# A windowed-attention block with an MLP: attention rewritten in unit slots, with projections and heads in groups of four units

## The reference

```python
h = layernorm(x, norm1_g, norm1_b)                 # over 48 channels
hw = windows(h)                                    # 1024 windows of 64 tokens
qkv = hw @ qkv_w + qkv_b                           # 3 heads of 16
attn = softmax((q * 16 ** -0.5) @ k.T + bias)      # bias by relative position
out = (attn @ v) @ proj_w + proj_b
x = x + unwindow(out)
h2 = layernorm(x, norm2_g, norm2_b)
return x + gelu(h2 @ fc1_w + fc1_b) @ fc2_w + fc2_b   # 192 hidden
```

## Time and profile before

| | us |
|---|---|
| median of 3 runs | 1205.87 |
| lowest and highest run | 1198.97, 1209.87 |
| profiled execution | 1205.63 |
| its span | 1203.9 |

### The profile page before, as it was taken

How to read it: one execution, slowest core, us unless ns; L and a number is a source line. 1 busy time by engine, 2 the same in 40 slices (tenths; PEclk the granted TensorE clock), 3 DMA queues, 4 the chain that set the end, 5 groups by cost and what they waited for, 6 DMA issues and landing times.

```text
span 1203.9 us, 29333 instructions
## 1 busy us (share of the span) xinstructions
PE 1079.1 (90%) x7622; PEld 964.3 (80%) x7622; DVE 873.9 (73%) x2751; ACT 896.8 (74%) x2755; POOL 759.7 (63%) x1173
## 2 busy tenths in 40 slices
PE   2998889888988889888889888888889999999997
PEld 1887777777777777777777777777779999999997
DVE  3567777777777777777777767777767777777773
ACT  2578777888888788888877888888777767667664
POOL 3555566565556656555566555556668888888882
PEclk9989999999999999999999999999989999999999
DMA  1000000100000010000000100000001111111111
GB/s 49 16 26 27 26 26 28 38 31 32 29 26 26 26 34 33 32 31 26 26 26 30 36 31 32 28 26 26 14 14 39 39 39 40 46 45 39 39 39 53
DMA packets 24744, 38.26 MB, mean 32 GB/s; under 512 B 4055, under 2 KB 20634, under 8 KB 24730
## 3 DMA queue, kind: packets, MB, share of 16 engines
q1 hardware_dynamic: 24730, 38.10, 10.0%
HBM read 25.50 MB, written 12.58 MB: 32 GB/s over the span
## 4 chain that ended last, share of the span: by engine, by line
PE 54%; ACT 23%; issue 12%; DVE 6%; POOL 3%; SPq 1%; DMA 1%; DVEq 0%; POOLq 0%; ACTq 0%
PE scores_ps L586 14%; ACT k_blocks L752 7%; PE kv_ps L509 4%; ACT v_blocks L763 4%; PE mixed_ps L539 4%; ACT tokens_t L740 4%; PE q_ps L515 4%; PE kv_ps L516 4%; ACT probs L768 3%; PE scores_ps L523 3%; PE turn_ps L550 3%; PE kv_ps L579 3%; PE turn_ps L563 2%; PE heads_t_ps L550 2%; POOL lowered L449 2%
## 5 line engine op out<-in xcount | busy, mean ns | idle before, releaser
L449 POOL TENSOR_TENSOR lowered<-biased,row_top 128x384 f32<-128x384 f32 x256 | 212.1, 828 | 355.0 <-DVE row_top L972 354.9
L523 PE MATMUL scores_ps<-k_blocks,q_blocks 96*128 96x192 f32 x1024 | 232.7, 351 | 42.2 <-DVE q_blocks L960 27.1
L752 ACT ACTIVATE k_blocks<-kv_ps 32x128 f32<-32x128 f32 x768 | 203.6, 265 | 64.0 <-PE kv_ps L516 58.0
L363 POOL TENSOR_TENSOR rstd<-small,minus_half 128x4 f32<-128x4 f32 (+1 forms) x160 | 243.3, 1527 | 0.0
L523 PEld LDWEIGHTS scores_ps<-k_blocks,q_blocks 96*128 96x128 f32 x1024 | 164.3, 194 | 64.2 <-issue 35.5
L968 DVE TENSOR_TENSOR biased<-scores_ps,pos 128x384 f32<-128x384 f32 x256 | 142.8, 558 | 96.1 <-PE scores_ps L523 89.9
L539 PEld LDWEIGHTS mixed_ps<-v_blocks,probs_t 128*128 128x128 f32 x1536 | 196.2, 195 | 15.6 <-issue 1.9
L539 PE MATMUL mixed_ps<-v_blocks,probs_t 128*128 128x66 f32 x1536 | 205.5, 271 | 0.9 <-ACT probs_t L745 0.9
L586 PEld LDWEIGHTS scores_ps<-wfc,hidden 128*128 128x128 f32 x1536 | 181.1, 192 | 5.4
L586 PE MATMUL scores_ps<-wfc,hidden 128*128 128x96 f32 x1536 | 179.9, 274 | 0.0
L972 DVE TENSOR_REDUCE row_top<-biased 128x6 f32<-128x384 f32 x256 | 141.6, 553 | 8.9
(11 more groups left out here) (106 smaller groups left out, 1888.2 us busy)
## 6 DMA issues: line engine op xcount, KB each, us to landing
x_in<-in_x SPq DMA_DIRECT2D x256, 48.0 KB
x<-in_x SPq DMA_DIRECT2D x128, 96.0 KB
out<-x SPq DMA_DIRECT2D x128, 96.0 KB
pos_in<-in_L_conv_rel_bias_table SPq DMA_DIRECT2D x8, 10.6 KB
wfc_in<-in_L_conv_fc_w SPq DMA_DIRECT2D x2, 36.0 KB
wqkv_in<-in_L_conv_qkv_w SPq DMA_DIRECT2D x2, 27.0 KB
wfc<-in_L_conv_fc_w SPq DMA_DIRECT2D x2, 24.0 KB
gains<-in_L_conv_norm_g SPq DMA_DIRECT2D x2, 0.2 KB
```

The lines of the kernel that those rows point to most:

```text
L363: pool.tensor_tensor(rstd[:, groups], small[:, 7, groups], minus_half[:, groups], ALU.pow).then_inc(step, 1)
L449: pool.tensor_tensor(lowered[:, k % 2, :, :], biased[:, k % 2, :, :], broadcast(row_top[:, k % 2, :], 2, TOK), ALU.subtract).then_inc(lowe ...
L523: mm = pe.matmul(bank[:, at:at + HEADS * TOK], q_blocks[:, k % 2, a, :, :].rearrange("p b q -> p (b q)"), k_blocks[:, k % 2, a, :, :].rear ...
L752: ins = act.activation(k_blocks[rows, k % 2, :, h, :], kv_ps[rows, at:at + 2 * TOK].rearrange("p (a t) -> p a t", a=2), ACT.Copy)
```

## The change

Attention is written anew on all engines; the MLP stage keeps its instructions and only takes other banks.

- Q, K and V are made for a group of four units: one matmul of 512 columns for Q, one for K, four for V. q_blocks, k_blocks and v_blocks hold two groups. `k_out` is three activations of 512 elements per group, `v_out` two of 384, `q_out` one of 1024.
- q_ps, kv_ps, turn_ps and heads_t_ps become four banks x_ps that rotate among the tokens, Q, K, V, transposed heads and the heads projection.
- `probs_t_out` is one activation of 384 elements.
- `normalise` is done for two units at once (a mixed_ps of two units), `turn_heads` and `heads_out` for four.
- In slot k TensorE does scores(k), turn_probs(k-2), one filling (`fill`), mix(k-2). ScalarE has exp(k-1) ahead of probs_t_out(k-2).
- GpSimd's preparation of the next batch begins in slot 6 of the batch before; SyncE loads x_in two batches ahead.
- wproj is loaded in the order of the new heads layout (six DMAs in place of two, and no masking on VectorE). The remaining preparation of weights moves from ahead of the first scores into slot 5 of the first batch.

The core of the diff; its `body` functions are, in this order, those of SyncE, GpSimd, TensorE, ScalarE and VectorE.

```diff
-        q_blocks = sb("q_blocks", [C2, 2, 2, 2, TOK])
-        k_blocks = sb("k_blocks", [C2, 2, 2, HEADS, TOK])
-        v_blocks = sb("v_blocks", [128, V_BUFS, HEADS, MIX])
+        q_blocks = sb("q_blocks", [C2, 2, UNITS, 2, 2, TOK])
+        k_blocks = sb("k_blocks", [C2, 2, UNITS, 2, HEADS, TOK])
+        v_blocks = sb("v_blocks", [128, 2, UNITS, HEADS, MIX])
...
+        x_ps = [ps(f"x_ps{i}") for i in range(4)]
+        turn2_ps = x_ps[1]
+        fc1_ps = [x_ps[2], x_ps[0], probs_t_ps]
...
+            sp.wait_ge(small_step, 10)
+            load_front(1)
+            def body(n, more):
+                if more:
+                    sp.wait_ge(small_step, FRONT_STEPS * (n + 1) + 10)
+                    load_front(n + 2)
                 wait(sp, x2_ok, 2 * n)
...
+            def body(n, first, last, more):
                 for k in range(QUADS):
                     lower(QUADS * n + k, k)
+                    if first and k == 1:
+                        front_sums(1)
+                        front_centre(1)
+                    if k == (2 if first else 0) and not last:
+                        front_root(0, 0)
+                        front_root(0, 1)
+                    if k == (2 if first else 1) and not last:
+                        front_root(1, 0)
+                        front_root(1, 1)
+                    if k == (3 if first else 2) and not last:
+                        front_scale(n + 1, 0)
+                        front_scale(n + 1, 1)
+                    if k == 6 and more:
+                        front_sums(n + 2)
+                    if k == 7 and more:
+                        front_centre(n + 2)
...
+            def project_q(bank, part):
+                pe.matmul(bank[0:C2, :], wqkv[:, 0:C2], group_tokens(part), start=True, stop=True).then_inc(q_mm, 1)
...
+            def fill(n, k, first, last):
+                if k == 0:
+                    wait(pe, x2_ok, 2 * n - 2)
+                    project_q(x_ps[0], 1)
+                    if not first:
+                        wait(pe, heads_ok, 4 * n - 2)
+                        turn_heads(x_ps[1], 0)
+                if k == 1:
+                    project_k(x_ps[2], 1)
+                if k == 2:
+                    wait(pe, v_ok, 2 * n + 1)
+                    project_v(x_ps[3], 1)
+                if k == 3:
+                    if not first:
+                        wait(pe, k_ok, 2 * n + 2)
+                        wait(pe, heads_ok, 4 * n)
+                        turn_heads(x_ps[2], 1)
+                    if not last:
+                        wait(pe, q_ok, 2 * n + 2)
+                        wait(pe, normed_ok, 2 * n + 3)
+                        turn_tokens(0)
+                        wait(pe, heads_t_ok, 2 * n - 1)
                         wait(pe, normed_ok, 2 * n + 4)
                         turn_tokens(1)
+                if k == 4:
+                    wait(pe, v_ok, 2 * n + 2)
...
+                        wait(pe, heads_t_ok, 2 * n)
+                        project_heads(x_ps[3], 0)
+                if k == 5:
...
+                        wait(pe, tokens_ok, 2 * n + 4)
+                        project_q(x_ps[1], 0)
+                        wait(pe, k_ok, 2 * n + 2)
+                        project_k(x_ps[2], 0)
+                if k == 6 and not first:
+                    project_heads(x_ps[0], 1)
+                if k == 7:
...
+                        wait(pe, x2_ok, 2 * n - 1)
+                        project_v(x_ps[3], 0)
+            def body(n, first, last):
+                s0 = QUADS * n
+                for k in range(QUADS):
+                    if k % UNITS == 0:
+                        wait(pe, q_ok, 2 * n + k // UNITS + 1)
+                        wait(pe, k_ok, 2 * n + k // UNITS + 1)
+                    wait(pe, biased_ok, s0 + k - 1)
+                    scores(k)
+                    if not (first and k < 2):
+                        turn_probs_of(s0 + k - 2, k)
+                    fill(n, k, first, last)
+                    if not (first and k < 2):
+                        wait(pe, probs_t_ok, s0 + k - 1)
+                        if k % 2 == 0:
+                            wait(pe, heads_ok, 4 * n + k // 2 - 1)
+                        if k == 2:
+                            wait(pe, v_ok, 2 * n + 1)
+                        mix(k - 2)
...
+            def k_out(part):
                 for h in range(HEADS):
                     rows = slice(2 * HD * h, 2 * HD * h + 2 * HD)
+                    ins = act.activation(k_blocks[rows, part, :, :, h, :].rearrange("p u a t -> p (u a) t"),
+                                         x_ps[2][rows, :].rearrange("p (ua t) -> p ua t", t=TOK), ACT.Copy)
                 ins.then_inc(k_ok, 1)
...
             def body(n, first, last):
+                s0 = QUADS * n
                 for k in range(QUADS):
+                    if not (first and k == 0):
+                        exp_of(s0 + k - 1, (k - 1) % QUADS)
                     if not (first and k < 2):
+                        wait(act, probs_turned, s0 + k - 1)
                         probs_t_out()
+                    if k == 0:
+                        wait(act, v_mm, 2 * n + 1)
+                        v_out(0)
+                    if k == 1 and not first:
+                        wait(act, heads_turned, 2 * n - 1)
+                        heads_out(x_ps[1], 0)
+                    if k == 2:
+                        wait(act, k_mm, 2 * n + 2)
+                        k_out(1)
+                    if k == 3:
+                        wait(act, v_mm, 2 * n + 2)
+                        v_out(1)
+                        if not first:
+                            wait(act, heads_turned, 2 * n)
+                            heads_out(x_ps[2], 1)
+                    if k == 4 and not last:
+                        for half in range(2):
+                            wait(act, turned, 2 * n + 3 + half)
+                            tokens_out(half)
+                    if k == 6:
...
+                            wait(act, k_mm, 2 * n + 3)
+                            k_out(0)
...
             def body(n, first, last, more):
+                s0 = QUADS * n
                 for k in range(QUADS):
+                    if k % 2 == 0 and not (first and k < 4):
+                        if k % UNITS == 0:
+                            wait(dve, heads_turned, 2 * n - 2 + k // UNITS)
+                        wait(dve, mixed_mm, s0 + k - 2)
+                        normalise(4 * n + k // 2 - 2, 1 - k // UNITS, k % UNITS)
+                    wait(dve, scores_mm, s0 + k + 1)
+                    top(s0 + k, k)
...
+                    if k == 1:
+                        wait(dve, q_mm, 2 * n + 2)
+                        q_out(x_ps[0], 1)
...
+                    if more and k in (4, 5):
+                        stats_front(n + 2, k - 4)
+                    if k == 5 and not first:
+                        dve.wait_ge(res_loaded, 64 * n)
+                        add_proj(n - 1, x_ps[3], 0)
+                    if k == 5 and first:
+                        other_weights()
+                    if k == 6:
...
+                            wait(dve, q_mm, 2 * n + 3)
+                            q_out(x_ps[1], 0)
+                    if k == 7 and not first:
+                        add_proj(n - 1, x_ps[0], 1)
```

More of the change, by code:

```diff
@@ L518, in scores, with project_k, project_v @@
+            def project_k(bank, part):
+                pe.matmul(bank[0:C2, :], wqkv[:, C2:2 * C2], group_tokens(part), start=True, stop=True).then_inc(k_mm, 1)
+            def project_v(bank, part):
+                for u in range(UNITS):
+                    mm = pe.matmul(bank[:, C2 * u:C2 * u + C2], tokens_t[:, UNITS * part + u, :], wqkv[:, 2 * C2:3 * C2],
+                                   start=True, stop=True)
+                mm.then_inc(v_mm, 1)
             def scores(k):
-                bank = scores_ps[k % 2]
+                part, u = divmod(k, UNITS)
@@ L630, in body @@
-                    if not (first and k < 3):
-                        if k == 3:
-                            wait(pe, x2_ok, 2 * n)
-                        turn_heads_of(g0 + k - 3, k - 3)
-                    if first and k == 2:
-                        wait(pe, weights_ok, 1)
-                    if not (first and k < 2):
-                        wait(pe, heads_ok, g0 + k - 2)
-                        mix(g0 + k - 2, k - 2)
-                    if k == 5 and not last:
-                        wait(pe, normed_ok, 2 * n + 3)
-                        turn_tokens(0)
@@ L646, in body @@
-                    if k == 5 and last:
+                if k == 4:
+                    wait(pe, v_ok, 2 * n + 2)
+                    if first:
+                        wait(pe, weights_in, 16 * WEIGHT_DMAS)
+                        pe.matmul(x_ps[3][:, 0:HID], fc1_shift[:, :], wfc1_in[0:C, :], start=True, stop=True
+                                  ).then_inc(bias_mm, 1)
+                    else:
```

(15 more changed lines are left out.)

419 lines of the change are left out of this document (153 added, 266 removed).

## The result

The changed kernel took 1118.01 us, median of 4 runs (1115.94 to 1121.09), beside 1202.42 us for the kernel before in the same series (4 runs, 1198.19 to 1209.87): ratio 0.929, 95% interval 0.924 to 0.935. The forecast was 1122 us. The profiled execution took 1117.6 us with a span of 1115.8.

The account below looks back on a forecast made before the run. Attention was taken as bound by TensorE's in-order queue plus its standstills. From 1205.6 us, 81 for steady batches and 2.6 for the start were subtracted, with nothing for drain and MLP: 1122 us, range 1095 to 1170.

Parts of the forecast that it names:

- The main term: Steady attention batches: period falls from 26.53 to 23.7 us, 2.8 us a batch over 29 batches, 81 us.
- The walk through the eight slots: Steady batch: slot lengths added up from instruction prices and latencies, carrying late engines over, sum 23.4 us.
- I add 0.3 for stops that the walk does not see: Steady batch: allowance of 0.3 us for unseen stops, raising the period from 23.4 to 23.7 us.
- Here GpSimd decides: Slot 3, turn of tokens: GpSimd's 13.4 us of work since slot 6 sets when tokens come; slot length 3.78 us.
- The ScalarE term: ScalarE in a steady batch: fewer, larger copies bring its work to 17.0 us; K from 3.2 to 1.8 per four units.
- 2.6 us won: Start: first biased 3 us later, but batch 0 then loses less; net 2.6 us won, bounds -6 and +5.
- The last batch and the drain keep their chains: End of attention: statistics, roots and transposes keep their chains, so no change, +-5 us.
- (a): Attention slots: late GpSimd or VectorE makes the exponential delay the probabilities' copy, 0.2 us a slot; period 25.2, 1164 us; chance 0.18.
- (b): Steady batches: the stalls go altogether, period near 22.5 us, total 1087 us; chance 0.07.
- (c): ScalarE's big copies cost 1108 ns like scattered 512-element writes; period 26.6, about 1203 us, no gain; chance 0.06.
- (d): Attention: new short stops make TensorE's clock fall once per batch, 4.3 us each; period 28.0, 1246 us; chance 0.09.
- The stop of VectorE for x_in: Sign of being wrong: VectorE waiting for input DMA at its statistics; lateness there was priced at nothing.

Follow-up runs that it names:

- Run 4: Changed kernel with Q and K of the next batch's first group projected and copied in slot 7 instead of slot 5: 1163.56 us, ratio 0.968.
- Run 3: Changed kernel with two of the four GpSimd roots per batch left out, so part of the tokens' normalisation is not computed: 1118.10 us, ratio 0.930.
- run 9: Changed kernel with only VectorE's copy of Q for the second group moved from slot 1 to slot 2: 1113.97 us, ratio 0.927.
- run 12: Changed kernel with the second group's Q copied in slot 2 and, in the drain, the last pair normalised before the rest of the second tokens: 1110.50 us, ratio 0.924.
- run 2: Changed kernel with K copied in twelve activations of 128 elements per group instead of three of 512: 1132.43 us, ratio 0.942.
- run 5: Kernel before with only larger ScalarE copies: K in three of 256 elements instead of six of 128, probabilities in one of 384: 1234.69 us, ratio 1.025.
- Run 7: Changed kernel with the second batch's statistics, sums, centring and first roots made before the first unit: 1117.07 us, ratio 0.930.
- the second profile: Changed kernel, unaltered, measured and profiled again in a later series: 1120.08 us, ratio 0.931.
- run 1: Changed kernel with ScalarE copying the transposed probabilities ahead of the exponential in each slot: 1125.71 us, ratio 0.936.
- run 8: Changed kernel with the second group's Q copied in slot 2 and centring moved from GpSimd to VectorE: 1126.22 us, ratio 0.938.

## Why the prediction was right, and where it was not

**The main term held, and was too small.** 81 us were predicted for the steady batches, 94.9 came. The walk through the eight slots was good: 23.38 us, measured 23.22 in the third batch (slots of 2.97, 2.52, 2.54, 3.84, 2.56, 3.56, 2.58, 2.65 against 2.97, 2.53, 2.64, 3.78, 2.62, 3.67, 2.60, 2.57). The term that was mis-sized is "I add 0.3 for stops that the walk does not see": there were none. With the 0.15 by which the walk itself is above the mean period of 23.25, mostly in slots 2 and 5, that is 29 x 0.45 = 13 us of the 13.9. Run 4 bears out the mechanism in the main: with Q and K made two slots later 46 us of the gain go. Single slots agree this closely in part by luck, since the next paragraph shows a wrong cause behind a right length.

**"Here GpSimd decides" was wrong, though its 3.78 us for slot 3 was nearly right.** Its list of GpSimd's work comes to 13.6 us by its own prices, not 13.4. Run 3 took two us of work from GpSimd and the steady batch did not get shorter. Runs 9 and 12 moved one VectorE instruction and some 0.15 us a batch went. The scaling stands behind a lowering that waits for VectorE's maximum, which stands behind normalising and the copy of Q. The forecast summed busy time where it should have followed the queue of the engine before.

**The ScalarE term was mis-sized.** K was priced "3.2 us in records and becomes 1.8"; in time it was 2.27 and is 1.77 (run 2). The forecast took no time from it, only room: beside the 17.0 us forecast for a batch, 133.82 / 200 x 23.25 = 15.6 were busy. Run 2 shows what the small copies of K would cost, 14 us in all. On the old order run 5 bounds what lighter copies give: 1.1 us a batch at full clock.

**The start, "2.6 us won", was +1.6,** in its bounds. The first scores start 3.7 us later (32.96 against 29.25), where 3 were forecast. The step forgot GpSimd's order in batch 0: four roots, 3.97 us, stand ahead of a lowering and the scaling, and TensorE waits 6.7 us for the first next tokens. Run 3, with two of these roots less, starts the third batch 2.5 us earlier. Run 7 removes the stop and wins 1.4 us by the third batch; 2.1 go to later first scores, and the clock is lower too, 0.86 in place of 0.89 on average from 30 us to the third batch.

**"The last batch and the drain keep their chains" was +4.9,** at the edge of its bounds, and +8.8 in the second profile. Heads are now normalised in pairs and turned in fours, so the last pair waits for the last mix, behind 1.39 us of other work on VectorE, and what follows runs at a clock of 0.73. Run 12, with that order swapped, has 804.44 - 761.79 = 42.7 us for this part and run 9 46.6: 3.9 us are the order. Why the part stays 2.6 us above the 40.0 of the kernel before is open.

The errors have both signs: -13.9 in the steady part, +4.2 and +4.9 at the edges, +0.3 in the MLP. They sum to -4.5, so the profiled execution, 1117.6, lies close to the forecast of 1122 in part because they cancel.

**The rivals.** (a) falls with the period and with run 1. (b), all stalls gone, came closer than (a): 23.25 lies between 22.5 and 23.7, and run 12 is at 23.10. (c) falls by its row: x192 of 583 ns. (d) did not come: the clock is 1.00 in the middle, with TensorE 98% busy. The Trainium skill (TensorE: Matmul & The Clock Gate, "A second HAM failure mode: psum-queue depth-cycling") reports, from a bf16 kernel that cycles through PSUM banks and idles briefly between groups, a clock that swings. This fp32 kernel has four rotating banks and stops of 0.4 us and less between its matmuls in the steady batches, and the clock stays up. Run 5, without the four banks and with stops of 1.17 to 1.73 us, is where it fell. So in these runs the falls go with longer stops and not with the four banks; but the kernel before also fell to 0.57 between 60 and 70 us without a stop above 0.8 in the 15 us ahead. What brings the clock down is open.

The stop of VectorE for x_in was named as what would make the forecast wrong. It came: 28.0 us in 26 stops, on the DMAs of the earlier trace rows. One stop of 11.3 stands ahead of the first scores, the others are about 0.7 us each. They cost nothing that the slots show: that an engine waits is no cost if it has room behind it. This sign of being wrong was badly chosen.

## What to carry to other kernels

When one engine runs in order and is nearly full, work made a group further ahead fills its short stops. Price the stops that are left by following the queue of the engine that releases them: what stands ahead of the releasing instruction there, and what ahead of that one's releaser. Busy sums said GpSimd; one VectorE instruction moved by a slot was the answer. And look at the first and the last batch by themselves: unrolled ends keep an order that was right for the old grouping, and here the clock was low behind their stops.

## What was not expected of the hardware

- Copies of 128 elements on ScalarE start 0.18 us apart though each record is 0.26 long (run 2); copies of 512 start 0.59 apart with records of 0.583. Sums of records overstate small copies.
- GpSimd's lowering took 1.39 us instead of 0.83 beside one VectorE subtraction with two inputs in SBUF (run 8).
- Making ScalarE's copies fewer slowed the kernel before by 2.5% (run 5): the batch was 1.1 us shorter at full clock, and the clock fell in eight places; the fall that is shown made its batch 6.7 us longer.
- In the drain a stop shortened by 1.4 us went with 3.9 us less, and a clock of 1.00 in place of 0.62 behind it (runs 9 and 12).
